# First attention of a two-layer block: one tile moved from the log path to the root path, and small work moved within a head

## The reference

```
q, k = l2norm(q), l2norm(k)
cos = q @ k.T
g_dist = arccos(clip(cos, -1 + 1e-7, 1 - 1e-7))
attn_score = (1 + g_dist) ** -3.2
n_r, n_c = sum(attn_score, rows), sum(attn_score, columns)
k_tilde = attn_score / n_r[:, None] / n_c[None, :]
out = (k_tilde / max(sum(k_tilde, -1), 1e-12)) @ v
```

## Time and profile before

| | us |
|---|---|
| median of 3 runs (3801.99 to 3806.85) | 3802.18 |
| the profiled execution, its own time | 3809.29 |
| its span | 3807.5 |
| busy: TensorE, ScalarE, VectorE, GpSimd | 3132.0, 3072.4, 2780.6, 2528.9 |

### The profile page before, as it was taken

One profiled execution on the slowest core, in us unless ns is written; L12 is line 12 of the kernel. 1 busy time (PEld: TensorE's weight loads), 2 busy tenths in 40 slices (PEclk: granted clock), 3 DMA queues, 4 the chain that ended last, 5 costly groups with the idle time before them and its releaser, 6 DMA issues. The chain is left out here.

```text
span 3807.5 us, 59074 instructions
## 1 busy us (share of the span) xinstructions
PE 3132.0 (82%) x19136; PEld 1280.5 (34%) x19136; DVE 2780.6 (73%) x3933; ACT 3072.4 (81%) x2642; POOL 2528.9 (66%) x1386
## 2 busy tenths in 40 slices
PE   4878887888888877878878676888888888888899
PEld 2321112211221112211211331555555555555547
DVE  6767886778767876778667996888778787788401
ACT  1799999999999999999998462888878788788822
POOL 2787877778787877778675241777767677777700
PEclk8776667766776677766776895999999999999999
DMA  0100000000000000000001253000110001100100
GB/s 28 46 7 7 6 0 6 6 6 0 6 6 6 4 2 6 6 6 0 6 10 32 72 162 83 24 24 24 41 30 23 24 24 41 29 23 24 38 0 12
DMA packets 59533, 85.67 MB, mean 22 GB/s; under 512 B 9808, under 2 KB 45904, under 8 KB 58960
## 3 DMA queue, kind: packets, MB, share of 16 engines
q1 hardware_dynamic: 59344, 83.06, 7.7%
HBM read 52.44 MB, written 30.54 MB: 22 GB/s over the span
## 5 line engine op out<-in xcount | busy, mean ns | idle before, releaser
L1176 POOL TENSOR_TENSOR lo<-pr,hi 128x1024 f16<-128x1024 f32 x384 | 916.8, 2412 | 389.5 <-ACT hi L1302 387.3
L1225 DVE TENSOR_REDUCE mx<-mx_ps 128x1 f32<-128x512 f32 x1024 | 660.4, 684 | 169.8 <-PE mx_ps L1340 166.3
L1317 ACT ACTIVATE pr<-s_ps 128x1024 f32<-128x1024 f32 x512 | 532.5, 1040 | 268.4 <-PE s_ps L1361 238.9
L1302 ACT ACTIVATE hi<-pr 128x1024 f16<-128x1024 f32 x512 | 548.3, 1072 | 0.0
L1340 PE MATMUL mx_ps<-ka,qa 128*128 128x512 f16 x1024 | 386.6, 399 | 141.8 <-DVE mx L1225 115.9
L671 ACT ACTIVATE wt<-wt 128x2048 f32<-128x2048 f32 x256 | 485.3, 1897 | 1.0
L471 POOL TENSOR_TENSOR base<-base,shift 128x1024 f32<-128x1024 f32 x160 | 303.5, 1897 | 255.9 <-DVE base L528 255.8
L662 ACT ACTIVATE wt<-wt,theta_bias 128x12288 f32<-128x12288 f32 (+4 forms) x80 | 459.7, 5747 | 0.2
L1380 PE MATMUL pv_ps<-vh,hi 128*128 128x129 f16 x4096 | 431.8, 222 | 11.0 <-ACT sums L1308 5.8
L1359 PE MATMUL s_ps<-qa,ka 128*128 128x512 f16 x1024 | 397.1, 388 | 38.9 <-issue 24.4
L1380 PE MATMUL pv_ps<-vh,lo 128*128 128x65 f16 x4096 | 417.6, 194 | 0.0
(11 more groups left out here) (194 smaller groups left out, 5257.1 us busy)
## 6 DMA issues: line engine op xcount, KB each, us to landing
qk<-stg SPq DMA_DIRECT2D x6, 2048.0 KB, 13.7
vh<-v SPq DMA_DIRECT2D x16, 520.0 KB, 3.5
qa<-qk SPq DMA_DIRECT2D x16, 512.0 KB, 3.5
ka<-qk SPq DMA_DIRECT2D x32, 256.0 KB, 4.8
v<-v_st SPq DMA_DIRECT2D x3, 2080.0 KB, 8.4
qst<-parts_dram SPq DMA_DIRECT2D x144, 32.0 KB
kst<-parts_dram SPq DMA_DIRECT2D x144, 32.0 KB
qk<-stg SPq DMA_DIRECT2D x4, 1024.0 KB, 8.3
```

The source lines that it names most:

```text
L1176: eng.tensor_tensor(lo[:, i % NHL, :, :], pr_slot(i), hi[:, i % NHL, :, :], ALU.subtract).then_inc(lo_done, 1)
L1225: eng.tensor_reduce(mx4[:, q // NCH, q % NCH:q % NCH + 1], mx_ps[:, q % 2, :], AX.X, ALU.max)\
L1302: eng.activation(hi[:, i % NHL, :, :], pr_slot(i), ACT.Copy).then_inc(hi_done, 1)
L1317: eng.activation(pr_slot(i), s_ps[:, i % 2, :, :], ACT.Exp, scale=SM).then_inc(exp_done, 1)
```

## The change

- `NL` is 5: eleven root tiles, five log tiles. The Sigmoids and Arctans work on pairs of log tiles, and the fifth tile goes alone (`PAIRS`).
- `GROUPS` has six groups: 5, 4, 3, 2, 1 and 1 places.
- In the ring the close of tile j comes behind the fold of tile j + 3 instead of j + 2, once it is wide; no close stands ahead of raise 5 any more. The slots of the last four chunks change.
- VectorE: `finish` from behind fold 1 to behind fold 4; `finish_rows` from ahead of raise 4 to behind the wide closes. Its clamp reads PSUM (`t_ps`) where it read `small`.
- TensorE: place 15 of the head before is weighed ahead of square 9 instead of square 4 (in the code, behind square 8 for square 3); `turn` behind the ring chunk of the third log tile; the turned factors go to `r_ps` and `m_ps` instead of `m_ps` alone; the first squares of the next head come behind place 11 instead of place 9.
- GpSimd: `products` from behind tile 4 to behind the last tile, beside `factors`.
- The plan's constants: `PRODUCT_US` 4.35 for 4.8, `LAG_US` 2.0 for 1.5.

```diff
-NL = 6
+NL = 5
...
-    GROUPS = (0, NL, NL + 4, NL + 7, NT - 1, NT)
+    GROUPS = (0, NL, NL + 4, NL + 7, NT - 2, NT - 1, NT)
...
-    NSG = NL // 2
+    PAIRS = tuple(range(0, NL, 2)) + (NL,)
+    NSG = len(PAIRS) - 1
...
-    wide = [(RA, FOLD)] + [(NQ + j, CLOSE) for j in range(NL)] + [(RA - 2, CLOSE)]
+    wide = [(RA, FOLD)] + [(NQ + j, CLOSE) for j in range(NL)]
     for j in range(RA + 1, NQ):
-        wide += [(j, RAISE), (j, FOLD), (j - 2, CLOSE)]
-    wide += [(NQ - 2, CLOSE), (NQ - 1, CLOSE)]
+        wide += [(j, RAISE), (j, FOLD), (j - 3, CLOSE)]
+    wide += [(j, CLOSE) for j in range(NQ - 3, NQ)]
     R1 = NCH * len(narrow)
     NRING = R1 + 2 * len(wide)
-    RE = NRING - 2
+    RS = NRING - 4
...
-    ROOT_US, CHUNK_US, PRODUCT_US, LOAD_US, LAG_US = 0.954, 0.625, 4.8, 1.3, 1.5
+    ROOT_US, CHUNK_US, PRODUCT_US, LOAD_US, LAG_US = 0.954, 0.625, 4.35, 1.3, 2.0
...
-        st_ps = m_ps[:, :, :].rearrange("p a b -> p (a b)").bitcast(F16)
         pair_ps = r_ps[:, :, :].rearrange("p a b -> p (a b)")
-        rc_ps = t_ps[:, 0, 0:NT].unsqueeze(2)
+        st_ps = (pair_ps.bitcast(F16), m_ps[:, 0, :].bitcast(F16))
+        rc_ps = t_ps[:, :, :].rearrange("p j (c r) -> p (j c) r", r=VC)[:, :, HD0 + 2:HD0 + 3]
...
                 for h in range(H):
-                    for j in range(RA + 1):
+                    for j in range(NQ):
                         shift_and_multiply(h, j)
                     if h + 2 < H:
                         eng.wait_ge(mono_ready, h + 2)
                         products(eng, sb, h + 2, mono)
-                    for j in range(RA + 1, NQ):
-                        shift_and_multiply(h, j)
-                    if h + 2 < H:
                         eng.wait_ge(fac_turned, 2 * h + 4)
                         factors(eng, sb, h + 2, mono, mono_ready)
...
-                    eng.tensor_tensor(quad[:, :, :, 1:2], rows_[:, :, :, HD0:HD0 + 1], quad[:, :, :, 0:1],
-                                      ALU.mult).then_inc(rows_done, 1)
+                    total = rows_[:, :, :, HD0:HD0 + 1]
+                    eng.tensor_tensor(total, total, quad[:, :, :, 0:1], ALU.mult).then_inc(rows_done, 1)
                     eng.wait_ge(rows_done, h * 5 + 2)
-                    eng.tensor_scalar(small[:, :, 1:2], small[:, :, 1:2], 1e-12, None, ALU.max).then_inc(rows_done, 1)
+                    eng.tensor_scalar(quad[:, :, :, 1:2], total, 1e-12, None, ALU.max).then_inc(rows_done, 1)
...
-                        if j == 1 and not first:
-                            finish(h - 1)
-                    if not first:
-                        finish_rows(h - 1)
                     raised(h, RA)
                     folded(h, RA)
+                    if not first:
+                        finish(h - 1)
                     for j in range(NL):
                         log_tile(h, j)
-                    closed(h, RA - 2)
                     for j in range(RA + 1, NQ):
                         raised(h, j)
                         folded(h, j)
-                        closed(h, j - 2)
+                        closed(h, j - 3)
+                    if not first:
+                        finish_rows(h - 1)
                     values(h, 0, GROUPS[1])
-                    closed(h, NQ - 2)
+                    closed(h, NQ - 3)
                     if not last:
                         for x in range(2):
                             stack(h + 1, x)
+                    closed(h, NQ - 2)
                     values(h, GROUPS[1], GROUPS[2] - GROUPS[1])
+                    values(h, GROUPS[2], GROUPS[3] - GROUPS[2])
                     closed(h, NQ - 1)
-                    values(h, GROUPS[2], GROUPS[3] - GROUPS[2])
                     values(h, GROUPS[3], GROUPS[4] - GROUPS[3])
                     values(h, GROUPS[4], 1)
+                    values(h, GROUPS[5], 1)
...
                     for p in range(NT):
-                        if p + 1 in GROUPS[1:4]:
+                        if p + 1 in GROUPS[1:NG]:
                             theta(h, GROUPS.index(p + 1))
-                        if p == NT - 1:
-                            theta(h, NG - 1)
                         score(h, p)
...
-                        if g == 3 and not first:
+                        if g == 8 and not first:
                             weigh(h - 1, NT - 1)
                         for r in range(done, ring_to[g]):
                             ring(h, r)
-                            if r == f_at(0) and not first:
-                                turn(h - 1)
                         done = max(done, ring_to[g])
-                    for r in range(done, RE):
+                    for r in range(done, RS):
                         ring(h, r)
-                    for p in range(3):
-                        weigh(h, p)
+                        if r == s_at(2) and not first:
+                            turn(h - 1)
                     if not last:
                         for x in range(2):
                             turn_factors(h + 1, x)
-                    for p in range(3, GROUPS[1]):
+                    ring(h, RS)
+                    for p in range(2):
                         weigh(h, p)
-                    ring(h, RE)
-                    ring(h, RE + 1, last)
-                    for p in range(GROUPS[1], GROUPS[2]):
+                    ring(h, RS + 1, last)
+                    for p in range(2, GROUPS[1]):
+                        weigh(h, p)
+                    ring(h, RS + 2, last)
+                    ring(h, RS + 3)
+                    for p in range(GROUPS[1], GROUPS[3]):
                         weigh(h, p)
                     if not last:
                         start(h + 1)
-                    for p in range(GROUPS[2], NT - 1):
+                    for p in range(GROUPS[3], NT - 1):
                         weigh(h, p)
```

More of the change, by code:

```diff
@@ L336, in stage_attention0 @@
     narrow += [(RA, RAISE)]
-    wide = [(RA, FOLD)] + [(NQ + j, CLOSE) for j in range(NL)] + [(RA - 2, CLOSE)]
+    wide = [(RA, FOLD)] + [(NQ + j, CLOSE) for j in range(NL)]
     for j in range(RA + 1, NQ):
-        wide += [(j, RAISE), (j, FOLD), (j - 2, CLOSE)]
-    wide += [(NQ - 2, CLOSE), (NQ - 1, CLOSE)]
+        wide += [(j, RAISE), (j, FOLD), (j - 3, CLOSE)]
+    wide += [(j, CLOSE) for j in range(NQ - 3, NQ)]
     R1 = NCH * len(narrow)
     NRING = R1 + 2 * len(wide)
-    RE = NRING - 2
+    RS = NRING - 4
+    assert (RS - R1) % 3 == 2
     ring_at = {step: NCH * i for i, step in enumerate(narrow)}
@@ L431, in slot @@
                 return r_ps[:, r % 2, :]
-            q = (r - R1) % 3 if r < RE else (2, 0)[r - RE]
+            q = (r - R1) % 3 if r < RS else (r - R1 + 2) % 3
             return m_ps[:, q, :] if q < 2 else pair_ps
@@ L503, in stack @@
                     eng.wait_ge(fac_turned, 2 * h + x + 1)
-                    eng.tensor_scalar(mst[:, x, :], st_ps[0:KM, cols(x, S)], -1.0 if x else 1.0, None, ALU.mult)\
+                    eng.tensor_scalar(mst[:, x, :], st_ps[x][0:KM, :], -1.0 if x else 1.0, None, ALU.mult)\
                        .then_inc(mst_ready, 1)
@@ L544, in log_tile @@
                 def log_tile(h, j):
-                    if j % 2 == 0:
-                        eng.wait_ge(sig_done, NSG * h + j // 2 + 1)
+                    if j in PAIRS:
+                        eng.wait_ge(sig_done, NSG * h + PAIRS.index(j) + 1)
                     for i in range(2):
@@ L683, in _ @@
                     for g in range(NSG):
-                        pair = wt[:, NQ + 2 * g:NQ + 2 * g + 2, :]
-                        eng.wait_ge(m0_read, NM0 * h + 2 * (NQ + 2 * g) + 4)
+                        pair = wt[:, NQ + PAIRS[g]:NQ + PAIRS[g + 1], :]
+                        eng.wait_ge(m0_read, NM0 * h + 2 * (NQ + PAIRS[g + 1]))
                         eng.activation(pair, pair, ACT.Sigmoid, scale=-0.5).then_inc(sig_done, 1)
                     for g in range(NSG):
-                        pair = wt[:, NQ + 2 * g:NQ + 2 * g + 2, :]
-                        eng.wait_ge(ring_read, NRING * h + s_at(2 * g + 1) + 2)
+                        pair = wt[:, NQ + PAIRS[g]:NQ + PAIRS[g + 1], :]
+                        eng.wait_ge(ring_read, NRING * h + s_at(PAIRS[g + 1] - 1) + 2)
                         eng.activation(pair, pair, ACT.Arctan, scale=1.0 / (GQK * GQK)).then_inc(atan_done, 1)
@@ L706, in turn_factors @@
                     if not (isinstance(h, int) and h == 0):
-                        eng.wait_ge(ring_read, NRING * (h - 1) + RE - 2 + x)
+                        eng.wait_ge(ring_read, NRING * (h - 1) + RS - 2 + x)
                     for i in range(NT):
-                        mm = eng.transpose(st_ps[0:KM, cols(NT * x + i)], fac[:, x, i, :], ident_h[:, :])
+                        mm = eng.transpose(st_ps[x][0:KM, cols(i)], fac[:, x, i, :], ident_h[:, :])
                     mm.then_inc(fac_turned, 1)
@@ L738, in ring @@
                     else:
```

(7 more changed lines are left out.)

## The result

The changed kernel takes 3673.47 us, the median of four runs (3669.9 to 3676.73), against 3802.09 for the kernel before: a ratio of 0.966 with a 95% interval of 0.9643 to 0.9676, or 129 us less. I had said 3698, with a range of 3676 to 3744. The time lies 2.5 us under the range.

What follows compares the result with a forecast made beforehand. ScalarE, running head into head, bounds the kernel: 112.6 us of work plus 3.4 of waits make 116.0 against 122.66; fifteen heads -100, the first -2, so 3700 from 3802.2. Laid-out times gave slightly less: 3698, range 3676 to 3744.

Steps and rivals of the forecast that it cites:

- Two places for a gain, ScalarE's work and its waits: Each head: a gain comes only from less ScalarE work (-3.3 us) or shorter waits (6.8 us before).
- finish_rows is the big wait, by the first head's 0.17: Before the last logs: moving finish_rows removes 4.5 us a head; the first head, without it, waits 0.17.
- The last weighting, 0.9: At the roots, ahead of square 9: a wait of 0.9 us, the cheaper of two earlier prices.
- 0.4 at the head's start, 0.6 for the small waits: 0.4 us for three weightings right before the last one; 0.6 for small root waits, 1.1 before.
- Arctan, 0.6: At the second arctan: shorter sigmoids make ScalarE wait 0.6 us for VectorE's eight chunks.
- Closing Lns, 0.3 + 0.3: Second half of a head: 0.3 us before the Ln of tiles 7 and 8, 0.3 at tiles 9 and 10.
- The sum: A head from the second on: 112.6 us of work plus 3.4 of waits, 116.0 against 122.66.
- The first head's -2: The first head, without the big wait: -3.3 us of work and 1.2 of new waits give -2.
- nothing waits: Rival: all new waits and the weighting are covered, 113.4 us a head, 3660; chance 0.07.
- my own case: The forecast of 3698 us itself: own range 3680 to 3716, chance 0.57.
- The late tail: Rival: closes 9 and 10 come 1.7 to 3.4 us late, by held clamp or slow weightings; 3732, chance 0.22.
- the low clock: Rival: TensorE's clock stays at 0.50 through the tail's weightings, 124.3 us a head, 3826; chance 0.04.

Runs made afterwards that it cites:

- e1: Kernel before with o_sb's copy behind fold 4, finish_rows behind the last fold and the turning behind the third log tile's ring chunk: 3744.1 us, ratio 0.983.
- e4: Changed kernel with the last weighting ahead of square 4 again: 3673.7 us, ratio 0.965 to the kernel before.
- e7: Changed kernel with the last weighting cut into its four matmuls, one ahead of each of squares 9 to 12: 3715.4 us, ratio 0.977 to the kernel before.
- e11: Changed kernel with the last weighting whole ahead of square 3, behind the squares that open the head: 3666.5 us, ratio 0.963 to the kernel before.
- e9: Changed kernel with five weightings, where two stood, between the ring chunks of tile 9's close: 3704.7 us, ratio 0.974 to the kernel before.
- e5: Changed kernel with the clamp of finish_rows on SBUF, as before: 3678.1 us, ratio 0.967 to the kernel before.
- e2: Changed kernel with o_sb's copy, finish_rows and the turning back in the narrow part, clamp still on PSUM: 3728.2 us, ratio 0.979 to the kernel before.

## Why the prediction was wrong, point by point

- *Two places for a gain, ScalarE's work and its waits.* Right. A settled head is 114.34 us, of which 1.96 are waits; the rest is work but for the 0.2 us of every second head: 112.3, for 112.6 foretold. The tile was priced right: from start to start sigmoids and arctans fall by 3.3 us (21.17 to 17.87) and the closing Lns rise by 0.07 (28.51 to 28.58). The 0.3 lies in the 32 chunks of roots and logs, which take 30.3 us for 30.7 without the waits, and which I had taken as equal.
- *finish_rows is the big wait, by the first head's 0.17.* Right: e1 gives 4.3 us a head and 61 us, with no wait at the logs; in the changed kernel there is one of 0.37, where I had 0.3.
- *The last weighting, 0.9.* Right in size: 0.94 + 0.17. That its new place brings the cheaper price was wrong: e4 has it at the old place for the same.
- *0.4 at the head's start, 0.6 for the small waits.* Both mis-sized: 0 of each in the settled head (0.17 is the weighting's tail). The three weightings end at 693.23 + 2.78 = 696.0, and square 3 is issued at 696.6. I had laid TensorE's tail too late: the seven weightings ahead of the next squares end at 685.68 + 6.21 = 691.89, which is 72.8 in the layout's time (its zero is 619.09, below), where I had about 75.
- *Arctan, 0.6.* 0.48.
- *Closing Lns, 0.3 + 0.3.* The first is 0, the second 0 and 0.2 in turn. These are the terms where the laid-out times were within 0.2 us of the line, and I charged a wait at each. For the Ln of tiles 7 and 8 close 8 came at 58.1 by the layout, and measured 58.0 (677.06, from the first sigmoids' end at 615.58 + 3.51 = 619.09), for an Ln that was wanted at 58.16 instead of 58.0. For tile 10 the error is the clock: I took the earlier trace rows's 5.3 slow us for the weightings alone, but TensorE is busy from the turning at 675.99 on and is at full clock after the first weighting in one kind of head, after the second in the other (3.64 us for the two).
- *The sum.* This is the step that failed: it had 3.4 us of waits where there are 1.96, or 2.05 with the 0.2 of every second head. That is some 1.35 of the 1.6 us a head by which heads 2 to 15 were off, and the work is the other 0.3: they fell by 8.26 where I had 6.7, 22 us in fourteen. The last head with its end brought 9.0 us (128.5 to 119.5 from its load to the last step of the rows) where I had 6.7; its last turning ran at full clock, 0.66 for 1.00 us. The first head's -2 was -2.2, in part by luck: in e7 and e11, whose edits don't touch it, it took 118.0 where the changed kernel's took 119.4.
- *The range.* Its lower end, 3676, took "nothing waits" (3660) as one case of 0.07 and my own case as ending at 3680. But the waits in the sum were each an upper guess, so the likely error was to one side. Four of seven terms at or near 0 is not a rival case. It belongs inside the forecast's own range: the four make 1.6 us a head, 15 x 1.6 = 24 us, and 3698 less 24 is 3674.
- *The rivals.* The late tail was near (e9: 1.3 us away), the clamp would not have brought it (e5, by luck of its start), and of the low clock only a trace came, the 0.2 us of every second head.

## What to carry to other kernels

When one engine runs without a break, split its time into work and waits, and price a wait by a place in the same trace where it is absent; the first iteration of a loop is often such a place. Small work on an engine that others wait for should stand where nothing is queued behind its reads, which here was worth 61 us by itself. When times laid out by hand come within their own error of each other, write the wait down as a range from zero and not as its upper end.

## What the runs showed of the hardware

- Four fp32 matmuls with 32 output columns each, to four parts of one accumulator, take 1.06 us together at full clock and 1.04 us one alone (e7). Cut into four pieces with other matmuls between them, the group cost ScalarE 3.27 us of waits a head for 1.11.
- A VectorE clamp of 16 values between SBUF operands took 0.18 us with GpSimd idle and up to 1.92 us otherwise, and ended with the GpSimd instruction that ran when it started (640.62 and 640.57; 673.27 and 673.23), within 0.05 us in 45 of 45 cases. With its source in PSUM it took 0.185 to 0.190 in all 16 heads, and 0.188 with 1.7 us of a GpSimd product to go (e2, at 1917.07).
- After 3.6 us without a matmul TensorE ran the squares and a weighting at half the pace (1.95 and 1.87 us, clock 0.56 from 608.66 to 611.96 of the kernel before); after 2.3 us without one, in the next head, at full pace (1.06 us, clock 1.00).
